# Inner pairs of the two field classes as two 64-column tiles in place of one 128-column operand, and table products for groups 1 and 2 alone

## The chip, the cores and the metric

One core of one Trainium2 chip runs the kernel. The metric is device time in microseconds for one execution, as the median of several. Five engines work side by side, each on its own queue of instructions: TensorE (PE, whose weight loads the profile lists apart as PEld), VectorE (DVE), ScalarE (ACT), GpSimd (POOL) and SyncE (SP, which here only issues transfers and passes on semaphores).

## The reference, cut to what matters

```python
e = jnp.stack([tbl_0[ids[:, 0]], ..., tbl_25[ids[:, 25]]], axis=1)      # (512, 26, 32)
x1 = einsum('bik,bjk,hij->bhk', e,  e, W1) + b1                         # h = 128
x2 = einsum('bik,bjk,hij->bhk', x1, e, W2) + b2
z  = sum(concatenate([x1, x2], axis=1), axis=-1)                        # (512, 256)
h  = concatenate([z, dense_ctx], axis=1)                                # (512, 272)
h  = maximum(h @ W_top1 + b_top1, 0); h = maximum(h @ W_top2 + b_top2, 0)
y  = h @ W_top3                                                         # (512, 1)
```

The tables 3, 5, 8 and 10 have 1000 rows of 32 numbers, the others up to 125000. All is float32.

## The kernel before, in words

**The second layer as triple products.** The sum over k of x2 needs, for each sample, the products of three embeddings, summed over the 32 numbers of each. The 26 fields are cut into two classes of 13. DVE writes into `l` the products of two fields: for each class 64 columns with the "inner" pairs (and squares, the 13 fields alone, a column of ones), and 42 columns with the pairs "across" the two parts of a class. `R` holds the 26 fields again, spread so that four samples stand side by side. TensorE multiplies a slice of `l` by a slice of `R` and thereby sums over k: that is `t_block`. A group of 128 samples has 32 slices. For the inner pairs a slice is one matmul of a 128-column operand (both classes beside each other) with 104 columns of `R` (L619); for the pairs across it is two matmuls with 42 columns each (L625, L626), each of which writes its own half of the partitions. A float32 matmul is issued as two instructions, each with a weight load ahead of it, so the inner pairs are 64 instructions a group and the pairs across 128. The profile writes 128x104 for 128 rows by 104 moving columns, and 128*128 or 128*42 ahead of it for rows by operand columns.

**Blocks and banks.** `t_block(g, n)` for n = 0 to 7 does four slices of inner pairs each, for n = 8 to 11 eight slices of pairs across. Each block fills one of three PSUM banks (`ring`); the list `turns` gives each user of the ring its bank, and the user three turns later waits until ScalarE (L803, L810, L811) or VectorE (L474, L478) has emptied it.

**The order within a group.** TensorE: the 12 blocks, then `z_group` (L655 inner, L660 across, L648 a part with the Gram matrix, which goes through DRAM), then two dense layers (L701 to L703, L711) for this group, then the blocks of the next group; the third layer (L722) stands behind block 1 of the next group. VectorE: `build_a(g)` transposes the first 13 fields out of `emb` into PSUM (L489), waits until all blocks of group g-1 are done (L492), copies (L494, L499) and multiplies (L503, L507); `build_b(g)` does the same for fields 13 to 23 and then 24 and 25. L507 has 18 instructions a class: 11 for the inner pairs, then 7 for the pairs across. TensorE's block 0 waits for all but the last seven.

**Where the embeddings come from.** GpSimd issues one indirect transfer (L317) for each group and field, in the order of groups and fields, into `emb`; SyncE waits for three parts of each group (fields 0 to 12, 13 to 23, 24 and 25; `PARTS`) and tells VectorE (`part_in`). The fields 3, 5, 8 and 10 of the groups from `OH_G` = 1 on are not fetched so. For these, VectorE makes a one-hot matrix of id // 8 (`one_hot`, L452, L456, from `octet_ids`, laid out by the host for 125 partitions), TensorE multiplies it by the small table (L639, `look_up`, two fields a turn, two turns a group: ahead of `z_group(0)` for group 1, behind blocks 4 and 6 of the group before for groups 2 and 3), and VectorE picks one of eight rows with a mask (`pick`, L474 and L478) and writes it to `emb`.

**Ahead of group 0** TensorE mixes the two weight tensors (L590), and VectorE assembles the operands of `z_group` from that (L397 to L444).

Of the kernel before, what the change touches and what calls it, by code (L numbers as in the profile page):

```python
# [17 lines left out]
I32 = mybir.dt.int32  # L18
# [3 lines left out]
P = 128  # L22
NF = 26
NH = NF // 2
K = 32
B = 512
G = B // P
# [9 lines left out]
HALF = 64  # L37
# [30 lines left out]
D1, D2 = 512, 256  # L68
OH = (3, 5, 8, 10)
OH_G = 1  # L70
OCT = 8
OR = 1000 // OCT
M1, M2 = D1 // P, D2 // P
# [14 lines left out]
def build(nc, a, y):  # L88
    with ExitStack() as ctx:
        def sb(name, shape, dt=F32):  # L90
            return ctx.enter_context(nc.sbuf_tensor(name, shape, dt))
# [49 lines left out]
        h1 = sb("h1", [P, M1, P])  # L141
        h2 = sb("h2", [P, M2, P])
        yrow = sb("yrow", [1, B])
        octet = sb("octet", [P, len(OH), B - OH_G * P], I32)
        onehot = octet[:, :, :].bitcast(F32)
        small_tbl = sb("small_tbl", [P, len(OH), OCT * K])
        place_in = sb("place_in", [P, G - OH_G, len(OH)], I32)
        place = sb("place", [P, G - OH_G, len(OH)])
        mask = sb("mask", [P, G - OH_G, len(OH), OCT])
        iota_p = sb("iota_p", [P, 1], I32)  # L150
        iota_pf = sb("iota_pf", [P, 1])
        iota_a = sb("iota_a", [P, OCT], I32)
# [80 lines left out]
        turns = [("pre", n) for n in range(EARLY)] + [("t", n) for n in range(TB)]  # L233
        def picks(g):

            return [("oh", (g - OH_G) * 2 + k) for k in range(2)] if OH_G <= g < G else []

        turns += [("pre", n) for n in range(EARLY, LATE)] + picks(1)
        turns += [("pre", n) for n in range(LATE, len(pre))] + [("z1", 0)]
# [23 lines left out]

        def rows_of(g, f0, f1):

            return sum(not (g >= OH_G and f in OH) for f in range(f0, f1))

        def lc(c, col, n):

# [33 lines left out]
        @block.gpsimd  # L303
        def _(pool):
            pool.memset(ident[:, :], 0.0).then_inc(ident_step, 1)
            pool.wait_ge(ident_step, 1)
            pool.affine_select(out=ident[:, :], in_=ident[:, :], compare_op=ALU.not_equal, fill=1.0, base=0,
                               pattern=[[-1, P]], channel_multiplier=1).then_inc(ident_step, 1)
            pool.iota(iota_p[:, :], pattern=[[0, 1]], base=0, channel_multiplier=1).then_inc(iota_ready, 1)
            pool.iota(iota_a[:, :], pattern=[[1, OCT]], base=0, channel_multiplier=0).then_inc(iota_ready, 1)  # L310
            pool.wait_ge(ids_in, 16)
            for g in range(G):
                for f in range(NF):
                    if g >= OH_G and f in OH:
                        continue
                    part = [c for c, (f0, f1) in enumerate(PARTS) if f0 <= f < f1][0]
                    pool.indirect_dma_start(  # L317
                        out=emb[:, g, f * K:(f + 1) * K], out_offset=None, in_=a[f"tbl_{f}"][:, :],
                        in_offset=bass.IndirectOffsetOnAxis(ap=idx[:, g, f:f + 1], axis=0),
                    ).then_inc(gathered[g][part], 16)  # L320

        @block.vector
        def _(dve):
# [122 lines left out]
            def one_hot():  # L446

                dve.wait_ge(iota_ready, 2)
                dve.wait_ge(octet_in, 16)
                dve.tensor_copy(iota_pf[:, :], iota_p[:, :])  # L450
                dve.tensor_copy(iota_af[:, :], iota_a[:, :])
                dve.tensor_scalar(octet[0:OR, :, :], octet[0:OR, :, :], 3, None, ALU.logical_shift_right).then_inc(octet_step, 1)  # L452
                dve.wait_ge(place_loaded, 16)
                dve.tensor_scalar(place_in[:, :, :], place_in[:, :, :], OCT - 1, None, ALU.bitwise_and).then_inc(octet_step, 1)
                dve.wait_ge(octet_step, 2)
                dve.tensor_scalar(onehot[0:OR, :, :], octet[0:OR, :, :], iota_pf[0:OR, 0:1], None, ALU.is_equal).then_inc(onehot_ready, 1)  # L456
                dve.tensor_copy(place[:, :, :], place_in[:, :, :]).then_inc(octet_step, 1)
                dve.wait_ge(octet_step, 3)
                n = (G - OH_G) * len(OH)
                dve.tensor_tensor(mask[:, :, :, :].rearrange("p g f a -> p (g f) a"),  # L460
                                  place[:, :, :].rearrange("p g f -> p (g f)").unsqueeze(2).to_broadcast([P, n, OCT]),
                                  iota_af[:, :].unsqueeze(1).to_broadcast([P, n, OCT]), ALU.is_equal).then_inc(octet_step, 1)
                dve.wait_ge(octet_step, 4)
# [99 lines left out]
        def _(pe):  # L563
# [43 lines left out]
            def t_block(g, n, first):  # L607
# [8 lines left out]
                if n < NB:  # L616
                    for i in range(BLK):
                        t = n * BLK + i
                        last = pe.matmul(ps[:, i * 4 * NF:(i + 1) * 4 * NF], l[:, t, 0:P],  # L619
                                         R[:, t, :, :].rearrange("p q f -> p (q f)"), start=True, stop=True)  # L620
                else:
                    for i in range(XBLK):
                        t = (n - NB) * XBLK + i
                        s = slice(i * 4 * NH, (i + 1) * 4 * NH)
                        pe.matmul(ps[0:NX, s], l[:, t, P:P + NX], R[:, t, :, NH:NF], start=True, stop=True)  # L625
                        last = pe.matmul(ps[HALF:HALF + NX, s], l[:, t, P + NX:LW], R[:, t, :, 0:NH], start=True, stop=True)  # L626
# [287 lines left out]
```

## Time and profile before

| | |
|---|---|
| median of 3 runs | 170.41 us (170.31 to 170.66) |
| the profiled execution's own time | 170.0 us |
| its span, first to last instruction | 168.1 us |
| mean granted TensorE clock over the span | 0.929 of full speed |
| TensorE busy | 137.4 us (82%) |
| VectorE busy | 111.0 us (66%) |
| GpSimd busy | 94.9 us (56%), 92 indirect transfers |
| ScalarE busy | 65.5 us (39%) |

Times within the profile are us from the start of the span; 1.9 us of the execution lie outside it. Busy time of TensorE counts matmuls that overlap once; how fast it really goes is read from the distance between the starts of two instructions.

### The profile page before, as it was taken

The numbers are of one execution on the slowest core, as the hardware profiler recorded it, in microseconds if no ns is written. First come the engines' busy times: TensorE is split into PE (matmuls) and PEld (weight loads), VectorE is DVE, ScalarE is ACT, GpSimd is POOL, SyncE is SP. The second block draws the span as 40 slices with busy tenths as digits, with TensorE's granted clock in tenths as the row PEclk, the third lists the DMA queues.
The fourth block names the chain that finished last, engine by engine and source line by source line (L and its number), as shares of the span: only waits on it lengthen the run. The fifth ranks groups of instructions, "written<-read, shape, count | busy, mean of one in ns | idle before, by whom it ended". The sixth has DMA issues, their size and how long they took to land.

```text
span 168.1 us, 3668 instructions
## 1 busy us (share of the span) xinstructions
PE 137.4 (82%) x1414; PEld 124.0 (74%) x1414; DVE 111.0 (66%) x425; ACT 65.5 (39%) x177; POOL 94.9 (56%) x100
## 2 busy tenths in 40 slices
PE   6418999200099979898899999899999979999995
PEld 6305666100099959788898899789899969999993
DVE  7899368999999919999804599980659996000000
ACT  1122888400025870350453730155281024574042
POOL 4778777787778777777777777777760000000000
PEclk9965999955559999999999999999999999999999
DMA  6994331000000312001011331010042000022000
GB/s 129 387 289 157 120 98 23 12 12 13 12 18 8 65 27 75 16 12 16 12 16 17 64 78 25 16 16 12 16 80 59 5 0 4 0 51 65 17 0 0
DMA packets 8537, 8.56 MB, mean 51 GB/s; under 512 B 3128, under 2 KB 7650, under 8 KB 8340
## 3 DMA queue, kind: packets, MB, share of 16 engines
q1 hardware_dynamic: 2668, 4.70, 8.8%
q10 hardware_dynamic: 2908, 2.12, 5.7%
q0 software_dynamic: 2944, 1.51, 5.3%
q8 instruction: 11, 0.18, 0.4%
q14 instruction: 6, 0.05, 0.1%
HBM read 7.28 MB, written 1.04 MB: 50 GB/s over the span
## 4 chain that ended last, share of the span: by engine, by line
PE 60%; DVE 16%; POOL 8%; ACT 6%; DMA 4%; issue 4%; ACTq 0%; DVEq 0%; SPq 0%
PE ring L619 15%; PE z2p L655 14%; POOL emb L317 8%; PE z2p L660 7%; PE ring L625 5%; PE h2y L711 4%; PE ring L639 4%; DVE l L507 3%; DMA emb<-in_tbl,idx 3%; DVE r L499 3%; DVE emb L478 3%; PE ring L648 2%; PE h1p L702 2%; ACT v_in L791 2%; DVE ctx_x L474 2%
## 5 line engine op out<-in xcount | busy, mean ns | idle before, releaser
L317 POOL DMA_INDIRECT emb<-in_tbl,idx x92 | 94.0, 1022 | 29.4 <-issue 27.7
L619 PE MATMUL ring<-r,l 128*128 128x104 f32 x256 | 32.7, 287 | 15.2 <-DVE l L507 15.2
L619 PEld LDWEIGHTS ring<-r,l 128*128 128x128 f32 x256 | 31.9, 203 | 16.3 <-DVE l L507 15.4
L803 ACT COPY t_in<-ring 128x416 f32<-128x416 f32 x32 | 16.2, 506 | 34.2 <-PE ring L619 34.2
L655 PE MATMUL z2p<-t_in,v_in 128*128 128x128 f32 x208 | 24.4, 277 | 0.8 <-ACT v_in L791 0.8
L655 PEld LDWEIGHTS z2p<-t_in,v_in 128*128 128x128 f32 x208 | 23.6, 192 | 1.2 <-ACT v_in L791 1.0
L590 PE MATMUL ring<-w1s,w2t 128*128 128x352 f32 x52 | 17.2, 494 | 4.0 <-DVE w1s L371 4.0
L590 PEld LDWEIGHTS ring<-w1s,w2t 128*128 128x128 f32 x52 | 10.6, 206 | 10.1 <-DVE w1s L371 4.1
L507 DVE TENSOR_TENSOR l<-sg_b,l 128x192 f32<-128x192 f32 (+5 forms) x72 | 15.6, 300 | 0.0
L507 DVE TENSOR_TENSOR l<-sg_a,l 128x192 f32<-128x192 f32 (+5 forms) x72 | 15.6, 298 | 0.0
L474 DVE TENSOR_TENSOR ctx_x<-ring,mask 128x512 f32<-128x512 f32 x6 | 4.1, 691 | 17.2 <-PE ring L639 17.1
L625 PE MATMUL ring<-r,l 128*42 128x52 f32 x256 | 13.0, 209 | 0.2
L626 PE MATMUL ring<-r,l 128*42 128x52 f32 x256 | 13.0, 209 | 0.0
L625 PEld LDWEIGHTS ring<-r,l 128*42 128x42 f32 x256 | 12.2, 117 | 0.9 <-DVE emb L478 0.5
L660 PE MATMUL z2p<-t_ac,v_ac 106*128 106x128 f32 x104 | 12.3, 275 | 0.0
L626 PEld LDWEIGHTS ring<-r,l 128*42 128x42 f32 x256 | 12.2, 117 | 0.0
L660 PEld LDWEIGHTS z2p<-t_ac,v_ac 106*128 106x128 f32 x104 | 12.0, 192 | 0.1
L499 DVE COPY r<-sg_b 32x352 f32<-32x352 f32 (+1 forms) x32 | 11.8, 369 | 0.3
L835 ACT ACTIVATE z<-z2p,kb 128x128 f32<-128x128 f32 x4 | 1.5, 367 | 24.1 <-PE z2p L660 21.6
L783 ACT COPY w_room<-ring 128x141 f32<-128x141 f32 x26 | 7.2, 278 | 7.5 <-PE ring L590 5.7
L499 DVE COPY r<-sg_a 32x416 f32<-32x416 f32 x16 | 9.4, 585 | 0.2
L784 ACT COPY mix<-ring 128x211 f32<-128x211 f32 x26 | 8.9, 341 | 0.0
(129 smaller groups left out, 183.3 us busy)
## 6 DMA issues: line engine op xcount, KB each, us to landing
w2t<-in_L_rec_W SPq DMA_DIRECT2D x1, 1664.0 KB, 7.2
emb<-in_tbl,idx POOLq DMA_INDIRECT x92, 2.4
wt<-in_W_top SPq DMA_DIRECT2D x2, 512.0 KB, 8.4
octet<-in_octet_ids SPq DMA_DIRECT2D x1, 750.0 KB
gram_scratch<-t_in ACTq DMA_DIRECT2D x4, 169.0 KB
gram<-gram_scratch ACTq DMA_DIRECT2D x4, 126.0 KB
small_tbl<-in_tbl SPq DMA_DIRECT2D x4, 125.0 KB
w<-in_L_rec_W SPq DMA_DIRECT2D x1, 338.0 KB, 7.7
```

Of the source, the lines that this page charges most:

```text
L317: pool.indirect_dma_start(out=emb[:, g, f * K:(f + 1) * K], out_offset=None, in_=a[f"tbl_{f}"][:, :], in_offset=bass.IndirectOffsetOnAxis( ...
L474: dve.tensor_tensor(masked, src, pair, ALU.mult).then_inc(masked_ready, 1)
L499: last = dve.tensor_copy(R[s, :, q, f0:f1], sgt[c][s, :, o:o + w])
L507: last = dve.tensor_tensor(lc(c, col, n), sgt[c][:, :, q:q + n], lc(c, SGL + p, 1).to_broadcast([P, NT, n]), ALU.mult)
L590: last = pe.matmul(ps[:, 0:PR + MIX], w2t[:, c, :], w1_of[c // NH], start=True, stop=True)
L619: last = pe.matmul(ps[:, i * 4 * NF:(i + 1) * 4 * NF], l[:, t, 0:P], R[:, t, :, :].rearrange("p q f -> p (q f)"), start=True, stop=True)
L625: pe.matmul(ps[0:NX, s], l[:, t, P:P + NX], R[:, t, :, NH:NF], start=True, stop=True)
L626: last = pe.matmul(ps[HALF:HALF + NX, s], l[:, t, P + NX:LW], R[:, t, :, 0:NH], start=True, stop=True)
L655: last = pe.matmul(zp[1], v_in[:, j, :], t_in[:, j, :], start=(start and j == j0), stop=(stop and j == j1 - 1))
L660: last = pe.matmul(zp[1], v_ac[0:MC, j, :], t_ac[0:MC, j, :], start=(start and j == 0), stop=(stop and j == NH - 1))
L784: last = act.copy(mix[:, c, :], ps[:, mixed:mixed + MIX])
L803: act.copy(t_in[:, :, n * 4 * BLK:(n + 1) * 4 * BLK], ps[:, 0:BLK * 4 * NF].rearrange("p (x j) -> p j x", j=NF)).then_inc(t_out, 1)
```

## The change

The inner pairs of a slice become two matmuls, one for each class: 64 columns of `l` each, with the same 104 columns of `R`, writing to the lower and the upper half of the partitions. Field values by table products are made for groups 1 and 2 only (`OH_E` = 3). Group 3 fetches its fields 3, 5, 8 and 10 by four more indirect transfers. `octet_ids`, `place_ids`, the one-hot matrix and the mask shrink from three groups to two.

```diff
+OH_E = 3
...
-        octet = sb("octet", [P, len(OH), B - OH_G * P], I32)
+        octet = sb("octet", [P, len(OH), (OH_E - OH_G) * P], I32)
...
-        mask = sb("mask", [P, G - OH_G, len(OH), OCT])
+        mask = sb("mask", [P, OH_E - OH_G, len(OH), OCT])
...
         def picks(g):
 
-            return [("oh", (g - OH_G) * 2 + k) for k in range(2)] if OH_G <= g < G else []
+            return [("oh", (g - OH_G) * 2 + k) for k in range(2)] if OH_G <= g < OH_E else []
...
         def rows_of(g, f0, f1):
 
-            return sum(not (g >= OH_G and f in OH) for f in range(f0, f1))
+            return sum(not (OH_G <= g < OH_E and f in OH) for f in range(f0, f1))
...
             for g in range(G):
                 for f in range(NF):
-                    if g >= OH_G and f in OH:
+                    if OH_G <= g < OH_E and f in OH:
                         continue
...
                     for i in range(BLK):
                         t = n * BLK + i
-                        last = pe.matmul(ps[:, i * 4 * NF:(i + 1) * 4 * NF], l[:, t, 0:P],
-                                         R[:, t, :, :].rearrange("p q f -> p (q f)"), start=True, stop=True)
+                        fields = R[:, t, :, :].rearrange("p q f -> p (q f)")
+                        s = slice(i * 4 * NF, (i + 1) * 4 * NF)
+                        pe.matmul(ps[0:HALF, s], l[:, t, 0:HALF], fields, start=True, stop=True)
+                        last = pe.matmul(ps[HALF:P, s], l[:, t, HALF:P], fields, start=True, stop=True)
```

TensorE's queue, the blocks 4 to 7 of group 2 before the change (L619 inner pairs, L639 the table products for group 3, L625 the first pair across; each row here is one matmul of the program, so two instructions of the profile):

```order
L619 MATMUL ring<-r,l 128x104 [waits t_out]
L619 MATMUL ring<-r,l 128x104 x3
L639 MATMUL ring<-small_tbl,octet 128x256 [waits t_out]
L639 MATMUL ring<-small_tbl,octet 128x256
L619 MATMUL ring<-r,l 128x104 [waits t_out]
L619 MATMUL ring<-r,l 128x104 x3
L619 MATMUL ring<-r,l 128x104 [waits t_out]
L619 MATMUL ring<-r,l 128x104 x3
L639 MATMUL ring<-small_tbl,octet 128x256 [waits picked_out]
L639 MATMUL ring<-small_tbl,octet 128x256
```

The same place after the change, the end of block 4 and block 5 (L622 and L623 are the two tiles of a slice):

```order
L623 MATMUL ring<-r,l 64x104
L622 MATMUL ring<-r,l 64x104 [waits t_out]
L623 MATMUL ring<-r,l 64x104
L622 MATMUL ring<-r,l 64x104
L623 MATMUL ring<-r,l 64x104
L622 MATMUL ring<-r,l 64x104
L623 MATMUL ring<-r,l 64x104
L622 MATMUL ring<-r,l 64x104
L623 MATMUL ring<-r,l 64x104
```

The two table products, with their waits, have gone from this group, and each slice has two matmuls where it had one. In group 1 the products stay where they were.

GpSimd's queue at the start of group 3 before the change (`in_tbl_N` is table N):

```order
81 L317 DMA emb<-in_tbl_0,idx 128x32
82 L317 DMA emb<-in_tbl_1,idx 128x32
83 L317 DMA emb<-in_tbl_2,idx 128x32
84 L317 DMA emb<-in_tbl_4,idx 128x32
85 L317 DMA emb<-in_tbl_6,idx 128x32
```

And after it:

```order
81 L318 DMA emb<-in_tbl_0,idx 128x32
82 L318 DMA emb<-in_tbl_1,idx 128x32
83 L318 DMA emb<-in_tbl_2,idx 128x32
84 L318 DMA emb<-in_tbl_3,idx 128x32
85 L318 DMA emb<-in_tbl_4,idx 128x32
86 L318 DMA emb<-in_tbl_5,idx 128x32
```

Up to number 83 the queue is the same; from there on tables 3, 5, 8 and 10 are put in, and the transfers of fields 13 to 25 stand four places later.

## Rows read from the trace of the kernel before

**Rows 1.** The page, busy time (share) and instructions by engine.

```profile
PE 137.4 (82%) x1414; PEld 124.0 (74%) x1414; DVE 111.0 (66%) x425; ACT 65.5 (39%) x177; POOL 94.9 (56%) x100
```

**Rows 2.** Timeline of PE, group 3: start, us, line, tiles, count.

```profile
140.25 1.93 PE L619 MATMUL ring<-r,l 128*128 128x104 f32 x16
142.10 0.60 PE L722 MATMUL h2y<-h,cols 128*1 128x128 f32 x4
142.63 5.61 PE L619 MATMUL ring<-r,l 128*128 128x104 f32 x48
148.17 0.24 PE L625 MATMUL ring<-r,l 128*42 128x52 f32 x1
151.27 6.07 PE L655 MATMUL z2p<-t_in,v_in 128*128 128x128 f32 x52
```

**Rows 3.** PE windows, L625 alone and L626 alone: stretch, length, busy (count).

```profile
148.17:150.43 2.26, 2.26 (x49) 2.26 (x50) 1.00 0.44 72
148.17:150.43 2.26, 2.26 (x48) 2.26 (x49) 1.00 0.44 72
```

**Rows 4.** PE: timeline, table products (with min/median/max ns) and group 0's blocks.

```profile
61.64 1.96 PE L639 MATMUL ring<-small_tbl,octet 125*128 125x256 f32 x8 [0.26 <-ACT v_ac L791]
L639 PE MATMUL ring<-small_tbl,octet x8: 379/379/454, 61.6 to 63.2; 125*128 125x256 f32 x8
45.86 9.48 PE L619 MATMUL ring<-r,l 128*128 128x104 f32 x64 [15.21 <-DVE l L507]
```

**Rows 5.** Windows: length, busy of PE, PEld, DVE, ACT, POOL (counts), PEclk, DMA, GB/s.

```profile
5.70:9.30 3.60, 0.90 (x6) 0.55 (x5) 2.99 (x13) 0.40 (x3) 2.75 (x3) 1.00 0.96 384
9.40:13.00 3.60, 0.00 (x0) 0.00 (x0) 3.53 (x33) 0.48 (x5) 2.69 (x3) 0.50 1.09 253
45.90:50.20 4.30, 4.30 (x20) 4.30 (x21) 4.30 (x32) 1.01 (x2) 3.39 (x4) 0.50 0.09 17
```

**Rows 6.** Chain that ended last, a transfer and group 2's blocks: start, us, what.

```profile
20.50 5.28 DMA emb<-in_tbl,idx
...
116.96 0.90 PE ring L639 x4
...
118.61 1.06 DVE emb L478
...
119.71 1.15 PE ring L639 x4
...
122.71 0.24 PE ring L625
```

**Rows 7.** Timeline of PE, where group 2's blocks begin and end.

```profile
111.64 1.93 PE L619 MATMUL ring<-r,l 128*128 128x104 f32 x16
125.07 0.38 PE L655 MATMUL z2p<-t_in,v_in 128*128 128x128 f32 x1
```

**Rows 8.** Timeline of DVE, group 0's and group 3's operands.

```profile
38.83 0.55 DVE L489 STREAM_TRANSPOSE sg_b<-emb 128x352 f32<-128x352 f32 x1
125.18 0.59 DVE L494 COPY l<-sg_a 128x416 f32<-128x416 f32 x1 [1.80 <-PE ring L626]
132.42 0.55 DVE L489 STREAM_TRANSPOSE sg_b<-emb 128x352 f32<-128x352 f32 x1
137.42 3.89 DVE L507 TENSOR_TENSOR l<-sg_b,l 128x192 f32<-128x192 f32 x18
```

**Rows 9.** POOL: two transfers of group 3, with the time to landing of the first; an early one.

```profile
121.61 0.95 POOL L317 DMA_INDIRECT emb<-in_tbl,idx  x1 [0.30 <-issue]
DMA to landing us min/median/max: 2.2/2.2/2.2
124.11 0.94 POOL L317 DMA_INDIRECT emb<-in_tbl,idx  x1 [0.30 <-issue]
23.00 1.74 POOL L317 DMA_INDIRECT emb<-in_tbl,idx  x1 [0.30 <-issue]
```

**Rows 10.** Timeline of DVE, second step of the one-hot matrix.

```profile
23.59 1.02 DVE L456 TENSOR_SCALAR octet<-octet,iota_pf 125x1536 f32<-125x1536 int32 x1
```

More of the change, by code:

```diff
@@ L143, in build @@
         yrow = sb("yrow", [1, B])
-        octet = sb("octet", [P, len(OH), B - OH_G * P], I32)
+        octet = sb("octet", [P, len(OH), (OH_E - OH_G) * P], I32)
         onehot = octet[:, :, :].bitcast(F32)
         small_tbl = sb("small_tbl", [P, len(OH), OCT * K])
-        place_in = sb("place_in", [P, G - OH_G, len(OH)], I32)
-        place = sb("place", [P, G - OH_G, len(OH)])
-        mask = sb("mask", [P, G - OH_G, len(OH), OCT])
+        place_in = sb("place_in", [P, OH_E - OH_G, len(OH)], I32)
+        place = sb("place", [P, OH_E - OH_G, len(OH)])
+        mask = sb("mask", [P, OH_E - OH_G, len(OH), OCT])
         iota_p = sb("iota_p", [P, 1], I32)
@@ L458, in one_hot @@
                 dve.wait_ge(octet_step, 3)
-                n = (G - OH_G) * len(OH)
+                n = (OH_E - OH_G) * len(OH)
                 dve.tensor_tensor(mask[:, :, :, :].rearrange("p g f a -> p (g f) a"),
@@ L899 @@
     inputs = dict(inputs)
-    by_field = _np.transpose(_np.asarray(inputs["ids"])[OH_G * P:, list(OH)])
+    by_field = _np.transpose(_np.asarray(inputs["ids"])[OH_G * P:OH_E * P, list(OH)])
     inputs["octet_ids"] = _np.broadcast_to(by_field, (OR,) + by_field.shape)
-    inputs["place_ids"] = _np.transpose(by_field.reshape(len(OH), G - OH_G, P), (2, 1, 0))
+    inputs["place_ids"] = _np.transpose(by_field.reshape(len(OH), OH_E - OH_G, P), (2, 1, 0))
     nc = _bacc.Bacc("TRN2", target_bir_lowering=False, num_devices=1)
```

## The prediction

> **What bounds the kernel now.** I read the page first: TensorE is busy 82% of the span, VectorE 66%, GpSimd 56% [rows 1]; none of the shares is so high that it settles the matter, the less as GpSimd's work all lies ahead of 125 us. The chain that ended last says which of these matters where. Up to the start of group 0's blocks it is GpSimd's first transfers and then VectorE: TensorE sat idle 15.21 us until 45.86, released by L507 [rows 4]. From there it is TensorE nearly throughout, in two kinds of stretch. The first kind are its own instructions back to back, such as all of group 3 from 140.25 to the end [rows 2]. The second is the table products of group 2: L639 at 116.96, then VectorE's L474 and L478 (1.06), then L639 again at 119.71, and block 9 released only at 122.71 [rows 6]. Third I read how much room the engines off the chain have, since a faster TensorE uses that up. VectorE starts group 3's operands at 125.18, when the last block of group 2 is done, and 137.42 plus 11 of 18 parts of 3.89 gives 139.8 at most for the inner pairs that block 0 waits for [rows 8], while TensorE comes there at 140.25 [rows 2]. Both count from the same event, the end of group 2's blocks (TensorE from 125.07, [rows 7]), so this half microsecond stays as it is when that event moves. GpSimd does not count from there: its transfers go out on a clock of their own, 1.25 us apart. The last of fields 13 to 23 of group 3 goes out at 121.61 and lands 2.2 later, the last of all goes out at 124.11 [rows 9]. VectorE wants fields 13 to 23 at 132.42 [rows 8]. So this room is 132.42 - 123.8 = 8.6 us.
>
> **The tiles.** At full clock 48 instructions of L619 take 5.61 us less the 0.27 that the last goes on: 47 distances of 0.113, or 0.112 without the pause at its start [rows 2]. The 128 columns of L655, with 128 moving columns where L619 has 104, go at 6.07 less 0.27 over 51, again 0.114 [rows 2]. More moving columns cost nothing, so L619 is bound by its weight load of 128 columns, 0.87 ns a column. The nearest row for two tiles side by side are L625 and L626: in 2.26 us 48 pairs start [rows 3], 0.047 a pair, each of the two with 42 weight columns and 52 moving ones. Serial weight loads at 0.87 ns a column would make 0.073 a pair, serial moving columns more than that: both are hidden behind each other. What one moving column costs where it binds shows L639 with 256: 1.96 less 0.38 to 0.45 over 7 is 0.216 to 0.226 [rows 4], 0.84 to 0.88 ns a column. The pair's own 0.047 / 52 is 0.90. So the new pair, bound by 104 moving columns, comes to 0.087 to 0.094; I take 0.090, and its 64 weight columns (0.056) are hidden. The gain is 64 x 0.0217 = 1.39 us a group at full clock. Bounds for the price of a pair: 0.087 below, 0.141 above, if each tile's weights wait for the other's moving columns (0.056 + 0.087 = 0.143 at most).
> The Trainium skill (TensorE: Matmul & The Clock Gate, Part 3, Packing small matmuls) says that weight loads overlap matmuls in flight only when the row group differs, and here both tiles use all rows. By that rule a pair would cost some 0.14 and the change would lose. L625 and L626 also use all rows and hide theirs, so the trace speaks against it at 42 columns.
>
> **Changing the tile shape.** Going from L619 to L722 or to L625 takes about 0.205 instead of 0.112 (the x16 group's last instruction starts at 140.25 + 1.93 - 0.27 = 141.91 and L722 at 142.10; the x48 group's at 147.97 and L625 at 148.17 [rows 2]). Before, a group changed shape at L722 (in and out) and at L625; afterwards at block 0 and at L722, and no more at L625. That is as many as before. Group 1 gets four more around its table products, 0.4 us, of which all but the first lie under the wait for VectorE.
>
> **Group by group.** Group 0 starts at half clock: 20 instructions in 4.30 us, 0.213 each [rows 5]. Moving columns bind there at twice the bare 0.087, some 0.174 a pair. If the clock comes back at the same moment, 25 pairs are done by then instead of 20, and the other 39 at 0.090 take 3.5: gain 1.4. Group 1: 40 of the 64 pairs stand ahead of its first table product and gain 0.87; what follows is the chain of L639 and VectorE (as [rows 6] shows for group 2), which does not move: 0.8. Group 2 loses its table products: its blocks took 125.07 - 111.64 = 13.43 [rows 7], and those of group 3, without products, 151.27 - 140.25 = 11.02 [rows 2]; so 2.4 from that and 1.4 from the tiles, 3.8. TensorE on its own would be at group 3's block 0 by 1.4 + 0.8 + 3.8 = 6.0 us earlier, at 134.2.
>
> **GpSimd.** Four more transfers stand ahead of fields 13 to 23 of group 3, 4 x 1.25 = 5.0 us: the last goes out at 126.61 and lands at 128.8. VectorE would want it at 132.4 - 6.0 = 126.4. The room of 8.6 is short of 5.0 + 6.0 by 2.4: VectorE waits, and TensorE behind it. From the transpose of these fields to block 0 it took 45.86 - 38.83 = 7.03 in group 0, where nothing else stood between [rows 4, 8]. So block 0 of group 3 starts at 128.8 + 7.03 and about 0.1 for SyncE to pass it on (my estimate), 136.0. GpSimd may be a little sooner: its transfer at 23.00 took 1.74 instead of 0.94, during L456 over 1536 columns at 23.59 [rows 9, 10], and there are 1024 columns now. I give it 0.2 of the 0.8 (bounds: 0 and 0.8, and as much the other way, since such delays depend on what VectorE does when). That makes 135.8, 4.45 earlier than 140.25. The last two fields go out at 129.1 and land by 131.5, just ahead of VectorE, 3.1 us behind the first transpose.
>
> **The sum.** 4.45 at the start of group 3's blocks and 1.39 within them: 5.84. The profiled execution took 170.0, so it would be 164.2; the median stands 0.4 above it, 164.6. Everything that groups 0 to 2 gain beyond 4.45 goes into the new wait, so their terms hardly matter, nor does an earlier landing of the smaller `octet` transfer. Other costs: VectorE loses the two passes of `pick` for group 3 and has its time back only as waiting.
>
> **Rivals.** (1) GpSimd isn't the bound: the extra fields are early enough, because its delays shrink or group 0 to 2 gain less than said. Then all 6.0 + 1.39 count: 163.0. For it speaks only that single transfers are held up, as the one at 23.00, and need not be; against it, that 1.25 us a transfer is the rule. (2) The clock falls in the new wait. TensorE idles there from about 134.2 to 135.8 or more. It fell after the stretch 5.70 to 9.30, in which TensorE was busy 0.90 of 3.60, and stood at half in the idle stretch behind it [rows 5]; the new idle stretch is about as long as the one ahead of that fall, or shorter. If it happens, some 20 pairs go at 0.174 and not 0.090, as many as went at half clock in group 0: +1.7, 166.3. (3) Transfers of group 3 land late, as the one at 20.50 did among the loads of the weights (5.28 and not 2.2, [rows 6]), or GpSimd is held up more: +1.5, 166.1. (4) The tiles gain nothing (0.112 a pair). Then group 2's 2.4 is all there is: 168.0. GpSimd has room for that (5.0 + 2.4 is under 8.6). (5) The other side: each tile's weight load waits for the other tile's moving columns, 0.141 a pair. That adds 64 x 4 x 0.029 = 7.4 and only 2.4 comes back: 175.4. It decides from 0.112 + 2.4 / 256 = 0.121 a pair on. Against it stands [rows 3].
>
> **How the numbers follow.** Forecast 0.64, rivals (1) 0.09, (2) 0.12, (3) 0.07, (4) 0.05, (5) 0.03. The time is that of the forecast, 164.6. The range of 163.2 to 166.4 holds the forecast with GpSimd 0.8 either way (163.8 to 165.4), (2), (3) and part of (1). Less than 0.2% (0.3 us) either way can't be told from no change. Faster: all but (5), less a little for (4), 0.96; the same 0.01; slower 0.03.
>
> **What the profile after would show.** Pairs of 64x104 start 0.090 us apart at full clock, two at once, and a group's inner pairs take some 5.8 us. Group 2's blocks take 9.6 us. 96 transfers, the last at about 129 us. In group 3 VectorE's transpose of fields 13 to 23 is released by SyncE at about 128.8 after idling some 2 us, and TensorE idles 1.5 to 2.5 us ahead of group 3's block 0, released by the last product of inner pairs. The prediction is wrong if that wait isn't there, if the pairs start more than 0.1 apart, or if the granted clock falls behind the wait.

## The result, and the profile after

| | before | changed |
|---|---|---|
| median | 170.36 us (169.71 to 170.66, 4 runs) | 163.29 us (163.09 to 164.21, 4 runs) |
| profiled execution, its span | 170.0 us, 168.1 us | 163.09 us, 160.9 us |
| mean granted TensorE clock over the span | 0.929 | 0.958 |

The ratio of the times is 0.9601 [0.9554, 0.9647]: the change takes 4.0% away. The time lies within the range, 1.3 us under the forecast of 164.6. A second measurement of the changed kernel gave 0.9596 [0.9544, 0.9648]. The ratios leave out executions that took over 1.5% longer than the shortest of the same kernel, which among the experiments concerns e1 alone, where it is two of four.

The page of the changed kernel answers to [rows 1]: busy time by engine, TensorE in tenths of 40 slices, the granted clock in tenths, and the chain that ended last by engine.

```profile
PE 131.3 (82%) x1662; PEld 117.0 (73%) x1662; DVE 106.8 (66%) x421; ACT 65.5 (41%) x177; POOL 96.8 (60%) x104
PE   6437999800099989798899999889999885999994
PEclk9999999985559999999999999999999999999999
POOL 57%; issue 18%; PE 15%; DVE 4%; DMA 3%; POOLq 1%; ACT 0%; DVEq 0%; SPq 0%
```

TensorE's share is 82% in both kernels. By that row the same engine limits the kernel as before. The chain says something else: it was TensorE for 60% of the span, and now it is GpSimd for 57% and "issue" for 18%, which is the 0.30 between two of GpSimd's transfers. A chain names the last arrival, by however little; how much it leads by is in the waits.

TensorE's timeline at the start of group 3's blocks, which answers to [rows 2]; the columns are start, duration, line, tile and count:

```profile
130.61 2.16 PE L714 MATMUL h2y<-h,wt 128*128 128x128 f32 x16 [0.46 <-ACT h L843]
134.59 0.30 PE L622 MATMUL ring<-r,l 128*64 128x104 f32 x1 [1.82 <-DVE l L508]
134.59 0.30 PE L623 MATMUL ring<-r,l 128*64 128x104 f32 x1
134.73 0.25 PE L622 MATMUL ring<-r,l 128*64 128x104 f32 x1
134.74 0.25 PE L623 MATMUL ring<-r,l 128*64 128x104 f32 x1
```

Two things are to be seen. The two tiles of a slice (L622 and L623) start together. And TensorE has nothing to do for 1.82 us ahead of block 0, where it had no wait before. The chain from GpSimd to that block (start, duration, what):

```profile
124.96 2.46 DMA emb<-in_tbl,idx
127.47 0.57 DVE sg_b L490
...
134.11 0.43 DVE l L508 x3
```

VectorE's timeline beside it. The first row is an earlier point, where group 2's blocks are over; it answers to the copy at 125.18 in [rows 8]:

```profile
117.54 0.59 DVE L495 COPY l<-sg_a 128x416 f32<-128x416 f32 x1 [2.49 <-PE ring L629]
...
127.47 0.56 DVE L490 STREAM_TRANSPOSE sg_b<-emb 128x352 f32<-128x352 f32 x1 [2.62 <-SPq L299]
...
130.62 0.24 DVE L490 STREAM_TRANSPOSE sg_b<-emb 128x64 f32<-128x64 f32 x1
```

VectorE idles 2.62 us until SyncE reports fields 13 to 23. The last two fields are there when it comes to them at 130.62. The transfers themselves:

```profile
124.96 0.94 POOL L318 DMA_INDIRECT emb<-in_tbl,idx  x1 [0.30 <-issue]
127.45 0.94 POOL L318 DMA_INDIRECT emb<-in_tbl,idx  x1 [0.30 <-issue]
```

The first of these rows is the last of fields 13 to 23; it lands 2.46 later. The second is the last of all 96. TensorE windows: the pairs of group 3 (L622 alone, 3.90 us), and the stretches ahead of and behind the wait's end with all engines. Columns as in [rows 5].

```profile
136.90:140.80 3.90, 3.90 (x46) 3.90 (x45) 1.00 0.01 4
132.20:134.50 2.30, 0.57 (x6) 0.38 (x4) 2.30 (x13) 0.62 (x2) 0.00 (x0) 1.00 0.00 0
134.60:141.00 6.40, 6.40 (x132) 5.99 (x134) 1.77 (x7) 3.89 (x8) 0.00 (x0) 1.00 0.01 3
```

From start to start a pair takes 0.0893 us at full clock. The granted clock is 1.00 (2.4 GHz) in the wait and behind it.

### The profile page after: what moved, and what is told of

Its sections match the earlier page's. It is cut to its first block, busy times and chain, and to the rows that moved or that the text cites. A ratio compares the mean times of both kernels' runs of the same rounds, so it can differ in the third digit from the quotient of the medians.

```text
span 160.9 us, 4161 instructions
## 1 busy us (share of the span) xinstructions
PE 131.3 (82%) x1662; PEld 117.0 (73%) x1662; DVE 106.8 (66%) x421; ACT 65.5 (41%) x177; POOL 96.8 (60%) x104
## 4 chain that ended last, share of the span: by engine, by line
POOL 57%; issue 18%; PE 15%; DVE 4%; DMA 3%; POOLq 1%; ACT 0%; DVEq 0%; SPq 0%
POOL emb L318 57%; PE z2p L658 4%; PE ring L622 4%; PE z2p L663 2%; DVE r L500 2%; PE ring L628 2%; DMA emb<-in_tbl,idx 2%; DMA idx<-in_ids 2%; DVE l L508 1%; POOLq L90 1%; PE h1p L714 1%; PE h2y L714 1%; PE ring L651 1%; DVE l L495 0%; DVE sg_b L490 0%
## 5 line engine op out<-in xcount | busy, mean ns | idle before, releaser
L318 POOL DMA_INDIRECT emb<-in_tbl,idx x96 | 96.0, 1000 | 30.8 <-issue 29.0
L622 PE MATMUL ring<-r,l 128*64 128x104 f32 x256 | 26.8, 266 | 14.7 <-DVE l L508 14.7
L622 PEld LDWEIGHTS ring<-r,l 128*64 128x64 f32 x256 | 25.0, 146 | 16.7 <-DVE l L508 15.1
L623 PE MATMUL ring<-r,l 128*64 128x104 f32 x256 | 26.8, 266 | 0.0
L623 PEld LDWEIGHTS ring<-r,l 128*64 128x64 f32 x256 | 25.0, 146 | 0.0
L591 PE MATMUL ring<-w1s,w2t 128*128 128x352 f32 x52 | 18.1, 514 | 3.5 <-DVE w1s L372 3.5
L628 PE MATMUL ring<-r,l 128*42 128x52 f32 x256 | 12.7, 208 | 0.3 <-DVE emb L479 0.3
L629 PE MATMUL ring<-r,l 128*42 128x52 f32 x256 | 12.7, 208 | 0.0
```

Source lines behind the costliest of these rows:

```text
L318: pool.indirect_dma_start(out=emb[:, g, f * K:(f + 1) * K], out_offset=None, in_=a[f"tbl_{f}"][:, :], in_offset=bass.IndirectOffsetOnAxis( ...
L591: last = pe.matmul(ps[:, 0:PR + MIX], w2t[:, c, :], w1_of[c // NH], start=True, stop=True)
L622: pe.matmul(ps[0:HALF, s], l[:, t, 0:HALF], fields, start=True, stop=True)
L623: last = pe.matmul(ps[HALF:P, s], l[:, t, HALF:P], fields, start=True, stop=True)
```

## The experiments

Each but e7 is an edit to the changed kernel, undoing a part of it or adding to it; where an edit adds lines, the line numbers of the rest move on. Ratios are to the kernel before, run on the same chip. Where a cause is sought, two profiles are compared, and each is one execution, so its tenths of a microsecond are no averages. In the profiles in which TensorE waits for GpSimd one relation returned: from the landing of fields 13 to 23 to block 0 of group 3 it takes 7.1 to 7.5 us.

**e1, the tiles alone.** The table products of group 3 come back, and with them the larger one-hot matrix.

```diff
-OH_E = 3
+OH_E = 4
```

> The two 64-column tiles as in the changed kernel, but table products for groups 1, 2 and 3, as before. My theory: GpSimd is not the bound here (its last transfers of group 3 go out at 124 us), TensorE is. The lookups cost group 2 their 2.4 us again, and with the larger one-hot input group 0's blocks start at about 45.9 us as before the change, not at 44.3. TensorE then reaches group 3's block 0 without waiting at 136 to 136.5 us: 164.8 to 165.2 us. Pairs start 0.089 us apart. Rival: the tiles brought little and the missing lookups brought the rest: 168 us or more.

Measured: 166.15 us (164.52 to 167.20), ratio 0.9731 [0.9674, 0.9787]. The ratio rests on the two shorter runs (164.52 and 165.31), which lie about the expected 164.8 to 165.2; by the medians of all runs it would be 0.979. Either way the case in which the tiles gain nothing is out. The profiled run (167.0) is one of the two longer. In it TensorE comes to group 3 without a wait, but at 138.76 and not at 136 to 136.5:

```profile
138.76 0.30 PE L622 MATMUL ring<-r,l 128*64 128x104 f32 x1
```

Group 2's blocks with their two turns of table products take 12.73 us, from 110.76 to 123.49, where they take 9.51 without (107.92 to 117.43 in the changed kernel). So these products cost 3.2, not the 2.4 of before. Most of the rest of the delay of group 3 lies between the starts of group 0 and group 1 (37.3 us, in the changed kernel 35.6), where ScalarE's queue holds a transfer's issue for 1.60 us, as in e7 below. Part of the 3.2 is that each change between tile shapes takes time: from a pair of tiles to L642 0.183 us and back 0.309, where the 128-column operand went back in 0.216.

**e2, fewer products alone.** One 128-column operand as before.

```diff
-                        pe.matmul(ps[0:HALF, s], l[:, t, 0:HALF], fields, start=True, stop=True)
-                        last = pe.matmul(ps[HALF:P, s], l[:, t, HALF:P], fields, start=True, stop=True)
+                        last = pe.matmul(ps[:, s], l[:, t, 0:P], fields, start=True, stop=True)
```

> Table products for groups 1 and 2 alone, as in the changed kernel, but the inner pairs as one 128-column operand, as before. My theory: group 2's blocks take 11.0 us and not 13.4, group 0's start comes about 1.6 us earlier with the smaller one-hot input, and GpSimd's transfers for group 3 land (127.4 us) just before VectorE wants them (128.4 us), so there is no wait: 166.3 to 166.8 us. Rival: the earlier start of group 0 is chance or is lost again, then 168.0 us. Second rival: GpSimd binds here already, then block 0 of group 3 is released by VectorE after a wait at 134.6 us, and the time is 164.7 us.

Measured: 166.61 us (166.06 to 167.48), ratio 0.9832 [0.9774, 0.989], as expected. TensorE comes to group 3 without a wait, though GpSimd has the same 96 transfers and sends the last at 127.5:

```profile
136.86 0.26 PE L622 MATMUL ring<-r,l 128*128 128x104 f32 x1
```

By the ratios the parts bring 2.7% and 1.7%, 4.4% in sum; together they bring 4.0%. The difference is within what the intervals leave open, and with all four runs of e1 the sum would be 3.8%, so the sum shows nothing of how the parts work on each other. The profiles do: only with both parts does TensorE wait for GpSimd.

**e3, two more transfers.** At the head of group 3's queue GpSimd fetches two fields once more into a spare tile, which SyncE waits for with the first part.

```diff
+        spare = sb("spare", [P, 2, K])
...
+                if g == G - 1:
+                    for f in range(2):
+                        pool.indirect_dma_start(
+                            out=spare[:, f, :], out_offset=None, in_=a[f"tbl_{f}"][:, :],
+                            in_offset=bass.IndirectOffsetOnAxis(ap=idx[:, g, f:f + 1], axis=0),
+                        ).then_inc(gathered[g][0], 16)
```

> The changed kernel with two more indirect transfers at the head of group 3, into a tile that nobody reads. My theory, that GpSimd's queue sets when group 3's blocks start: both transfers' 1.25 us show in full, +2.5 us, 165.8 us, and TensorE idles 4.4 us ahead of group 3's block 0 in place of 1.9. If the granted clock falls in that longer wait, up to 1.7 us more. Rival: the queue has room and TensorE is the bound: 163.3 us.

Measured: 167.53 us (166.7 to 168.41), ratio 0.9896 [0.983, 0.9962]. TensorE's timeline, and windows ahead of and behind the wait's end:

```profile
136.89 0.44 PE L629 MATMUL ring<-r,l 128*64 128x104 f32 x1 [4.34 <-DVE l L515]
```

```profile
131.00:136.80 5.80, 1.55 (x14) 1.35 (x12) 5.65 (x23) 0.74 (x3) 0.00 (x0) 1.00 0.02 3
136.95:140.30 3.35, 3.35 (x35) 2.93 (x36) 1.74 (x7) 0.82 (x2) 0.00 (x0) 0.50 0.00 0
```

Block 0 starts 2.3 us later than in the changed kernel, and the last transfer goes out 2.3 later (129.77 and 127.45): GpSimd is the bound there. On top of that the granted clock is 0.50 (1.2 GHz) from 136.95 on for 3.4 us, after a stretch in which TensorE worked 1.55 of 5.80 us. From block 0 to the end it takes 27.9 us instead of 26.3. The two parts, 2.3 and 1.6, make the 3.9 by which the profiled executions differ (167.0 and 163.1). In the changed kernel, after a wait of 1.82 where this is one of 4.34, the clock stayed.

**e9, the same with TensorE kept busy.** As e3, and 18 matmuls on an identity ahead of the wait.

```diff
+            keep_warm(18)
```

> The kernel with two more transfers for group 3, plus 18 matmuls that nobody needs (36 instructions, about 4.0 us) on TensorE ahead of group 3's block 0, where it idled 4.4 us. With the two transfers alone the granted clock fell to half at 136.92 us, as group 3's blocks began, and stood there for 3.4 us. My theory: that fall is paid for by 1.6 us beside the 2.5 us of the transfers; with TensorE busy in the wait the clock stays, block 0 still starts at 136.9 us, and the time is 165.7 to 166.2 us. Rival (the clock's fall is cheap, the excess comes from elsewhere): 167.2 us or more.

Measured: 167.28 us (166.18 to 168.14), ratio 0.9869 [0.9817, 0.992].

```profile
133.56 4.18 PE L576 MATMUL h1p<-ident 128*128 128x128 f32 x36
137.67 0.30 PE L629 MATMUL ring<-r,l 128*64 128x104 f32 x1
```

```profile
137.70:144.00 6.30, 6.30 (x131) 5.89 (x132) 0.68 (x3) 3.80 (x8) 0.00 (x0) 1.00 0.01 3
```

The clock stays at 1.00, and from block 0 to the end it takes 26.3 us again. Between these two profiles, then, the idle time brought the clock down in e3, and the fall cost 1.6. The times don't show it: the median of e9 lies above the forecast (165.7 to 166.2) and just within the rival's range, and by the ratios e9 and e3 can't be told apart. Part of the reason is that VectorE was ready at 136.57 and the 36 instructions ran on for 1.1 us past that, and the profiled execution (166.18) is the shortest of the four.

**e5, the tiles half by half.** The four lower tiles of a block first, then the four upper ones, to see whether two tiles run side by side only when neighbours in the queue use different halves.

```diff
-                        pe.matmul(ps[0:HALF, s], l[:, t, 0:HALF], fields, start=True, stop=True)
-                        last = pe.matmul(ps[HALF:P, s], l[:, t, HALF:P], fields, start=True, stop=True)
+                        pe.matmul(ps[0:HALF, s], l[:, t, 0:HALF], R[:, t, :, :].rearrange("p q f -> p (q f)"), start=True, stop=True)
+                    for i in range(BLK):
+                        t = n * BLK + i
+                        s = slice(i * 4 * NF, (i + 1) * 4 * NF)
+                        last = pe.matmul(ps[HALF:P, s], l[:, t, HALF:P], R[:, t, :, :].rearrange("p q f -> p (q f)"), start=True, stop=True)
```

> The changed kernel with the same tiles in another order: within a block the four slices of the lower half first, then the four of the upper half, so that neighbours in the queue use the same 64 columns of the array. My theory: two tiles run at once only where neighbours in the queue use different columns, and each costs its 0.089 us of moving columns; a block of inner pairs takes 1.3 to 1.4 us in place of 0.72, a group 5 us more, and TensorE is the bound again from the first group on: 178 to 182 us. Rival (TensorE looks far enough ahead to pair them up anyway): 163.3 us, with pairs 0.089 us apart. Second rival (weights of 64 columns that can't be hidden behind a matmul on the same columns): 0.14 us an instruction, over 195 us.

Measured: 167.14 us (166.21 to 167.96), ratio 0.9823 [0.9756, 0.9891]. All three theories missed, mine by more than 10 us. TensorE's timeline at group 3 (L621 the lower tiles, L625 the upper):

```profile
137.81 0.66 PE L621 MATMUL ring<-r,l 128*64 128x104 f32 x5
138.22 0.30 PE L625 MATMUL ring<-r,l 128*64 128x104 f32 x1
138.30 0.25 PE L621 MATMUL ring<-r,l 128*64 128x104 f32 x1
138.36 0.25 PE L625 MATMUL ring<-r,l 128*64 128x104 f32 x1
138.39 0.25 PE L621 MATMUL ring<-r,l 128*64 128x104 f32 x1
```

In the program eight lower instructions stand in a row and then eight upper ones. On the chip the first upper one starts after five lower ones, and from there on the halves work side by side; further on, lower tiles of the next block start beside upper ones of this block. A block takes 0.83 us against 0.72, the inner blocks of a group 7.58 against 6.43. The order in the queue thus costs far less than two tiles one after another would, because the upper half is taken up out of turn. Where the 0.11 a block goes isn't settled: one half is alone only at the start and the end of such a row of blocks, and in between some distances within a half are 0.15 us among those of 0.09.

**e4, one turn of table products for group 3.** Fields 3 and 5 by products, 8 and 10 by transfers, to split the load between GpSimd and TensorE.

```diff
-OH_E = 3
+TURNS = 5
...
+        def by_table(g, f):
+            return g >= OH_G and f in OH and (g - OH_G) * 2 + OH.index(f) // 2 < TURNS
```

> The changed kernel with one turn of table products for group 3 (fields 3 and 5) and transfers for fields 8 and 10 only. My theory: GpSimd is 2.5 us earlier with group 3 and no longer the bound by 132.1 us; TensorE alone would be at block 0 of group 3 at 132.7 us plus 1.0 to 1.3 for the one turn, so 133.7 to 134.0 in place of 134.6: 162.3 to 162.7 us. Rival (TensorE's or VectorE's path was the bound all along, and one more lookup turn costs what it costs): 164.3 us or more.

Measured: 163.69 us (163.31 to 164.91), ratio 0.9651 [0.9613, 0.9688]: not better than the changed kernel, and between my range and the rival's. GpSimd is done earlier, with the last transfer at 125.83. TensorE doesn't wait any more in the profiled execution (164.91, the longest of the five), but it is there only at 136.51:

```profile
136.51 0.30 PE L625 MATMUL ring<-r,l 128*64 128x104 f32 x1
```

Group 2's blocks take 11.21 us with one turn, against 9.51 with none: 1.7 for a turn, where I had taken 1.0 to 1.3. Another 0.9 is a later start of group 0 (45.17), and 1.2 lie between the starts of group 0 and group 1, with the long issue of e7 among them (1.67).

**e6, the one-hot matrix at its old size.** Its ids and VectorE's passes over them cover three groups again; only two are used.

```diff
-        octet = sb("octet", [P, len(OH), (OH_E - OH_G) * P], I32)
+        octet = sb("octet", [P, len(OH), B - OH_G * P], I32)
```

> The changed kernel, but the one-hot input and the one-hot matrix keep their three groups (1536 columns, 750 KB); the third is not used. My theory for the 1.2 us by which group 3's block 0 came earlier than I predicted: the smaller transfer and VectorE's shorter steps hold GpSimd up less and let the first embeddings land earlier. So here GpSimd's delays add up to 6.6 to 7.0 us again in place of 5.4, its last transfer goes out at 128.7 to 129.1 us, and the time is 164.5 to 165.0 us. Rival (chance of phase between the two engines): no difference beyond 0.3 us, 163.0 to 163.6 us.

Measured: 164.14 us (163.44 to 164.68), ratio 0.9662 [0.9606, 0.9718]. That is between the two ranges (164.5 to 165.0, and 163.0 to 163.6), but every run is longer than every run of the changed kernel beside it (e7), so it is no chance. GpSimd's timeline, and VectorE's beside it:

```profile
21.55 1.73 POOL L318 DMA_INDIRECT emb<-in_tbl,idx  x1 [0.30 <-issue]
```

```profile
22.14 1.02 DVE L457 TENSOR_SCALAR octet<-octet,iota_pf 125x1536 f32<-125x1536 int32 x1
```

While this operation runs a transfer takes 1.73 and not 0.94. All delays of GpSimd, which are the distances between its transfers over 1.25 summed, come to 6.4 us (5.6 in the changed kernel run beside it), and the last transfer goes out at 128.43 (127.55). The median is 0.95 us longer, the transfer 0.88 later. Group 0 starts at 45.26, 0.9 later than with the small matrix (44.32). So GpSimd's path and TensorE's own are both 0.9 later here. VectorE waits 1.05 us for fields 13 to 23, and TensorE hardly waits for VectorE:

```profile
135.46 0.30 PE L622 MATMUL ring<-r,l 128*64 128x104 f32 x1 [0.26 <-DVE l L508]
```

e6 thus shows what the size of the matrix is worth, some 0.95 us of the change's gain, but not which of the two paths is the bound.

**e7, the changed kernel again,** beside e6 and e8.

> The changed kernel itself, for comparison on this chip: 163.3 us, group 3's block 0 after a wait at 134 to 135 us, no other difference.

Measured: 163.19 us (162.46 to 163.40), ratio 0.9596 [0.9544, 0.9648]. The median is the same, but the wait ahead of group 3 has all but gone:

```profile
134.67 0.30 PE L622 MATMUL ring<-r,l 128*64 128x104 f32 x1 [0.22 <-DVE l L508]
```

Block 0 starts where it did (134.59), and VectorE has waited 1.02 us for fields 13 to 23, but TensorE came there 1.7 later. Of that 0.7 is group 0's inner blocks, in which the clock stood at half for longer (ScalarE's first copy of a block across starts at 53.75, in the first profile at 53.03). The other 1.0 is ScalarE, whose queue (ACTq) held a transfer's issue for 1.61 us while TensorE waited for its copies:

```profile
54.10 1.61 ACTq L820 DMA_DIRECT2D gram_scratch<-t_in  x1
55.75 0.50 ACT L813 COPY t_ac<-ring 42x416 f32<-42x416 f32 x1 [0.99 <-issue]
```

In the first profile of the changed kernel that issue took 0.39. So there are two paths to block 0, and in these two profiles TensorE's own ends 0.2 and 1.8 us before the other.

**e8, GpSimd's delay at the ninth transfer taken away.** The zeroing of half of `R`, 1.45 us on VectorE during that transfer, is done by GpSimd itself while it waits for the first ids.

```diff
+            pool.memset(R[:, NT // 2:NT, :, :], 0.0).then_inc(zeroed, 1)
...
-            dve.memset(R[:, NT // 2:NT, :, :], 0.0).then_inc(zeroed, 1)
```

> The changed kernel, with the second half of R zeroed by GpSimd while it waits for the indices, in place of VectorE's 1.45 us at 13.9 us. If GpSimd's queue is the bound, what holds it up counts: its ninth transfer took 2.55 us in place of 0.95 while VectorE ran that zeroing and the split of the weights behind it. My theory: that delay shrinks by 1 to 1.4 us, and the zeroing costs GpSimd at most 0.5 us at its start: 162.3 to 163.0 us. Rival: GpSimd's own zeroing of 1664 columns is slow (over 2 us) and delays all transfers: 163.5 to 165 us; either way the time moves with the moment of GpSimd's last transfer.

Measured: 162.81 us (162.12 to 163.33), ratio 0.9573 [0.9518, 0.9629].

```profile
1.59 1.48 POOL L312 MEMSET r<- 128x1664 f32 x1
...
13.43 0.94 POOL L319 DMA_INDIRECT emb<-in_tbl,idx  x1 [0.30 <-issue]
```

```profile
134.68 0.30 PE L622 MATMUL ring<-r,l 128*64 128x104 f32 x1
```

The ninth transfer takes 0.94 (2.55 in the changed kernel, while the memset ran), all delays sum to 3.8 and the last transfer goes out 1.8 earlier. The time lies within the range, but the time was to move with GpSimd's last transfer, and the profile doesn't bear that out: block 0 still starts at 134.68, now without a wait, so TensorE was no sooner there. The median is 0.4 below that of e7, and the intervals overlap. The issue on ScalarE's queue took 1.88 us here, and later the clock stood at half once more, over 3.4 us, after 2.83 us of work in the stretch from 52 to 56 and 1.52 in that from 56 to 58.3:

```profile
52.91 1.88 ACTq L820 DMA_DIRECT2D gram_scratch<-t_in  x1
```

```profile
58.30:61.70 3.40, 3.28 (x10) 2.40 (x9) 0.46 (x1) 1.37 (x4) 2.79 (x3) 0.50 0.20 40
```

In this profile GpSimd's gain became room.

**e10, the issue moved.** The store of the Gram matrix's part, `gram_out(0)`, is issued behind all of ScalarE's copies for the blocks across, not between them.

```diff
-                if n == NB:
-                    gram_out(0)
...
+            gram_out(0)
```

> The changed kernel with ScalarE's two store transfers of group 0's Gram rows issued behind its copies for v_ac, in place of between the blocks' copies. In the executions in which the second of these issues coincided with VectorE's wide additions (L445) it held ScalarE for 1.6 to 1.9 us in place of 0.39, and TensorE waited 1.1 to 1.4 us for a bank behind it. My theory: this stall goes, TensorE comes 1.1 us earlier to group 3's block 0, but finds GpSimd's embeddings missing until 134.6 us as before: 163.0 to 163.3 us, the same as the changed kernel on this chip within 0.3 us. Rival (TensorE's path is the bound in these executions): up to 1 us faster, 162.2 us.

Measured: 163.46 us (163.40 to 163.62), ratio 0.9627 [0.9593, 0.9662]: no gain. TensorE has its time back, and waits with it:

```profile
135.06 0.30 PE L622 MATMUL ring<-r,l 128*64 128x104 f32 x1 [1.72 <-DVE l L508]
```

**e11, e8 and e10 together.**

> Both: the second half of R zeroed by GpSimd, and the store of group 0's Gram rows issued later. With the zeroing alone GpSimd's last transfer went out at 125.7 us and not 127.5, and TensorE no longer waited ahead of group 3's block 0, yet the block began at 134.7 us as before, since TensorE itself came late (1.4 us of that behind ScalarE's long issue). My theory: two bounds lie within half a microsecond of each other, and only taking both away shows: block 0 at 133.2 to 134.0 us, 161.7 to 162.4 us. Rival: a third thing binds at the same moment (VectorE's path, about 0.6 us short of TensorE's): 162.8 us, as with the zeroing alone.

Measured: 162.37 us (161.29 to 162.78, 6 runs), ratio 0.9555 [0.9513, 0.9596].

```profile
126.66 0.56 DVE L491 STREAM_TRANSPOSE sg_b<-emb 128x352 f32<-128x352 f32 x1 [2.33 <-SPq L299]
...
133.76 0.30 PE L622 MATMUL ring<-r,l 128*64 128x104 f32 x1 [1.53 <-DVE l L509]
```

Fields 13 to 23 are there 0.8 us earlier than in the changed kernel, and block 0 starts 0.8 earlier. GpSimd is still what it waits for; its last transfer goes out at 126.73, only 0.7 earlier than in the changed kernel, where e8 had gained 1.7. Every run lies below every run of e10 on the same chip, which has TensorE's repair alone, so with that repair in place an earlier GpSimd counts. Against the changed kernel itself the intervals meet (0.9555 [0.9513, 0.9596] and 0.9601 [0.9554, 0.9647]), and the two weren't run beside each other; nor can e11 be told from e8 (0.9573 [0.9518, 0.9629]). So e11 has the lowest ratio of all, and that it beats the changed kernel is likely but not settled.

## Why the prediction was right, and where it was off

**The pair: right.** Forecast 0.087 to 0.094, taken 0.090; measured 0.0893, and 0.173 at half clock (forecast 0.174). That pairs are bound by their 104 moving columns was read off the 42-column tiles and L639, and it held. The Trainium skill (TensorE: Matmul & The Clock Gate, Part 3, Packing small matmuls) says in its list of what overlaps that weight loads do so only when the row group differs, though the text ahead of it also lets them go to a background weight buffer. These tiles share all rows, and the trace disagrees with the list: by that rule a pair would take about 0.14, an estimate from the rows of the kernel before.

**The tiles' gain in the groups: close.** Group 2's blocks took 9.51 (forecast 9.6). Group 0's inner blocks took 7.80 us against 9.42, from their start to the first pair across, a gain of 1.6 (1.4 forecast). Group 1 gained 0.68 (0.8 forecast). From block 0 of group 3 to the end it took 26.3 us where the forecast had 26.5.

**TensorE's own arrival: 1.4 too late.** I had it at 134.2; it was ready at 132.8. What was missing is the start of group 0, 44.27 instead of 45.86 [rows 4]. The smaller one-hot matrix does that: with the old size it is 45.26 (e6) or 45.42 (e1). The step said that an earlier landing would hardly matter, as it goes into the new wait. That was right for the first profile. In e7 this 1.6 makes up for most of the slow issue on ScalarE's queue and the longer time at half clock (1.7 together), and without it block 0 would have been late.

**GpSimd as the new bound: right.** VectorE's wait for fields 13 to 23 and TensorE's behind it stand in the profile as described, 2.62 and 1.82 us. e2, with the same 96 transfers and a slower TensorE, has no wait. e3 moves block 0 with the transfers, and e11 starts it 1.3 earlier than e10, its last transfer being 0.9 earlier. e6 moves both paths and decides nothing here. But the margin is small: where ScalarE's issue is slow, TensorE arrives 0.2 ahead of VectorE (e7), or VectorE ahead of it (e8). The prediction would have been wrong by its own sign without the wait of 1.5 to 2.5 us, and the second profile of the same kernel has 0.22. That the first has 1.82 is in part luck: nothing in the working foresaw the slow issue.

**The term that was mis-sized is GpSimd's delays.** I took 1.25 a transfer from the last ones of before, and 0.2 off for a shorter L457, with 0.8 as the bound. The last transfer went out at 127.45 where this gives 129.1 - 0.2: 1.5 earlier, and 1.66 against the undiminished sum. The sum of the delays fell from 7.05 to 5.35 us. Transfer by transfer the 1.7 is four pieces of some 0.4. One comes straight from the smaller one-hot matrix: the transfer beside its second step was late by 0.39 and not 0.79 (0.78 in e6, 0.25 to 0.65 in the other profiles with the small matrix), so here I gave 0.2 where 0.4 was due, within the bound of 0.8. The other three I hadn't thought of, and they come and go with the moment at which VectorE's operations fall. The sixth transfer took 1.40 before and 1.02 after, but 1.40 again in the changed kernel's second profile. Three around 35 us lost 1.25 in sum and then 0.80, but 1.24 again in e5 with the small matrix. The 34th lost 0.48 and then next to nothing, but 0.49 again in e6, and 0.48 in e9 with the small matrix. By e6 and e7 the size of the matrix is worth 0.8 to 0.9 of GpSimd's time by all its ways together; that the rest fell on the helpful side is luck. Against it stands a landing of 2.46 instead of 2.2. Together block 0 came at 134.59 and not 135.8, which is 1.2 of the 1.3 us by which the time is below the forecast. The other terms nearly cancel: 0.2 less from block 0 to the end than forecast (26.3 and 26.5) and 0.2 less from the profiled execution to the median (0.4 before, 0.2 after), against 0.3 more of the execution outside the span (1.9 before, 2.2 after).

**The rivals.** (1) was half of it: GpSimd did run earlier, but was still the bound. (2) did not happen here; the profiles of e3 and e9 show that it is real and costs 1.6 (1.7 forecast), after a wait of 4.34 us where the changed kernel had one of 1.82. (3) and (4) and the other side, (5), are out.

## What to carry to other kernels

A matmul that is bound by the columns of its weights became cheaper as two tiles side by side with half the columns each, both writing to their own half of the partitions and issued in turn; the price was then that of the moving columns (0.112 us down to 0.0893 with 128 weight and 104 moving columns). When an engine on the path is made faster, work out when the feeder with a clock of its own (here GpSimd, 1.25 us a transfer) comes to the same place, and count its delays from VectorE's operations one by one, since they were the largest error here. When two paths end together, a repair to either can show nothing: in the profiles neither e8 nor e10 started the block earlier, and both together did, by 0.8 us.

## What the runs showed of the hardware

**VectorE can hold up GpSimd's transfers.** In the changed kernel one took 2.55 us, while a memset over 128x1664 (1.45 us) and then two operations that split weights ran, in e6 one took 1.73 during a pass over 125x1536; undisturbed ones take 0.94. e8 takes the memset away and the 2.55 becomes 0.94, though the same split then runs beside the transfers. But the memset doesn't always do it. In e9 it ran at the same place, and the two transfers beside it took 0.94 and 1.29:

```profile
13.92 0.94 POOL L325 DMA_INDIRECT emb<-in_tbl,idx  x1 [0.30 <-issue]
13.93 1.45 DVE L552 MEMSET r<- 128x1664 f32 x1 [0.30 <-issue]
```

In e3 the same two start at 13.93 and 13.94, and the transfer takes 2.54. What decides isn't shown. The Trainium skill (SBUF — State Buffer, SBUF: two separate sides) describes such a hold: VectorE's wide modes lock the port by which GpSimd writes a transfer's descriptors. The 1.73 of e6 agrees with it; of a memset that section says nothing.

**An issue on ScalarE's queue took 0.39 or 1.6 to 1.9 us.** It is the second of two that store a part of the blocks' result for the Gram matrix (L820). It took 0.39 in the kernel before, in the changed kernel's first profile and in e2, 0.51 in e3, and 1.6 to 1.9 in e1 and e4 to e9, and TensorE lost 1.0 to 1.4 us behind it. At its later place in e10 and e11 it took 0.39. I first laid it to VectorE's addition over 128x637 (L445, L446 in e8), which in the slow cases ran during the issue. The first profile of the changed kernel and e8 speak against that:

```profile
53.39 0.39 ACTq L820 DMA_DIRECT2D gram_scratch<-t_in  x1
53.91 0.82 DVE L445 TENSOR_TENSOR vh_in<-vh_in,w_room 128x637 f32<-128x637 f32 x1
```

```profile
53.44 0.82 DVE L446 TENSOR_TENSOR vh_in<-vh_in,w_room 128x637 f32<-128x637 f32 x1
```

The addition begins 0.52 after the issue in the first and 0.53 after it in e8, GpSimd's next transfer 0.69 and 0.70 after it, and one issue takes 0.39, the other 1.88. With an issue of 0.39 the addition of e8 would have begun after its end too. In e9 the same issue was slow in group 3 too, 1.66 us from 145.41 on, when GpSimd's last transfer (129.50) and VectorE's last work were long over. So what lies beside it on these engines doesn't decide, and the cause stays open.

**Tiles in different halves overtake each other.** In e5 an upper tile starts after five of eight lower ones that stand ahead of it in the queue.

**Changing the tile shape costs time.** From 128 to 64 columns it takes 0.205 us until the next start, from a pair of tiles to 128 columns with 256 moving ones 0.183 and back 0.309; from tiles of 64 to tiles of 42 columns nothing (0.083).
